# A recommendation tower: 17 gathered features instead of 16 in the first block, nine looked-up ones instead of ten

## What is computed

```python
combined = jnp.concatenate([dense_features[:, None, :], sparse_features], axis=1)   # (2048, 27, 128)
interactions = jnp.einsum('bfd,bgd->bfg', combined, combined)
interactions_flat = interactions[:, _IU0, _IU1]
z = jnp.concatenate([dense_features, interactions_flat], axis=1)
h = jnp.concatenate([z, r_dense_features], axis=1)
h = jnp.maximum(h @ W_top1 + b_top1, 0.0)
h = jnp.maximum(h @ W_top2 + b_top2, 0.0)
y = h @ W_top3
```

## Time and profile before

| | |
|---|---|
| median of 3 runs | 372.1 us (370.02 to 376.62) |
| the profiled execution's own time | 367.56 us |
| its span, first to last instruction | 365.8 us |
| PE busy | 339.0 us (93%) |
| DVE, POOL busy | 258.8 us each (71%) |
| ACT busy | 200.2 us (55%) |
| granted clock of PE, mean | 0.995 |

### The profile page before, as it was taken

How to read it: one execution, slowest core, us unless ns; L and a number is a source line. 1 busy time by engine, 2 the same in 40 slices (tenths; PEclk the granted TensorE clock), 3 DMA queues, 4 the chain that set the end, 5 groups by cost and what they waited for, 6 DMA issues and landing times.

```text
span 365.8 us, 8218 instructions
## 1 busy us (share of the span) xinstructions
PE 339.0 (93%) x3392; PEld 278.4 (76%) x3392; DVE 258.8 (71%) x190; ACT 200.2 (55%) x276; POOL 258.8 (71%) x268
## 2 busy tenths in 40 slices
PE   0889989999889799999999999999999999999987
PEld 0657668888778588888878688888877787868876
DVE  2969999899999979979787549878895221302132
ACT  2799995565549246654645454734636275734200
POOL 6778777777778777777777777777777777772220
PEclk9999999999999899999999999999999999999999
DMA  7998935599998559789535556787556431544310
GB/s 186 261 260 219 266 97 157 133 255 271 244 248 197 143 135 246 215 214 222 163 91 128 156 142 198 187 218 170 115 151 160 129 77 50 150 116 103 92 20 3
DMA packets 38034, 60.26 MB, mean 165 GB/s; under 512 B 20626, under 2 KB 21612, under 8 KB 37998
## 3 DMA queue, kind: packets, MB, share of 16 engines
q1 hardware_dynamic: 29046, 42.94, 44.8%
q0 software_dynamic: 8256, 16.42, 18.5%
q10 hardware_dynamic: 696, 0.38, 0.3%
HBM read 49.47 MB, written 10.23 MB: 163 GB/s over the span
## 4 chain that ended last, share of the span: by engine, by line
PE 67%; ACT 11%; SPq 8%; DMA 5%; issue 5%; DVE 4%; ACTq 0%; DVEq 0%
PE look_bank L790 29%; PE short_bank L887 13%; PE out_bank L821 8%; PE out_bank L837 6%; PE short_bank L872 5%; ACT one_hot L929 4%; PE out_bank L832 4%; ACT high_table L918 2%; SPq L656 2%; SPq L667 2%; DMA whole_table<-in_tbl 2%; ACT one_hot L936 2%; DVE one_hot L1111 2%; PE out_bank L849 1%; DMA block_scratch<-all_dots 1%
## 5 line engine op out<-in xcount | busy, mean ns | idle before, releaser
L730 POOL DMA_INDIRECT rows<-in_tbl,all_ids x248 | 251.8, 1015 | 77.1 <-issue 74.4
L1111 DVE TENSOR_TENSOR one_hot<-spread_ids,row_bank 128x2048 fp32r<-128x2048 int32 (+2 forms) x87 | 182.0, 2132 | 16.2 <-PE look_bank L790 11.9
L790 PE MATMUL look_bank<-one_hot,high_table 125*128 125x512 f32 x348 | 145.8, 419 | 18.2 <-DVE low_table L1099 11.3
L790 PE MATMUL look_bank<-one_hot,low_table 125*128 125x512 f32 x348 | 137.9, 396 | 0.0
L790 PEld LDWEIGHTS look_bank<-one_hot,high_table 125*128 125x128 f32 x348 | 66.7, 192 | 37.9 <-DVE low_table L1099 10.4
L790 PEld LDWEIGHTS look_bank<-one_hot,low_table 125*128 125x128 f32 x348 | 66.9, 192 | 15.7 <-issue 2.6
L887 PEld LDWEIGHTS short_bank<-all_combined 128*59 128x59 f32 x2048 | 57.9, 133 | 11.3 <-issue 9.7
L887 PE MATMUL short_bank<-all_combined 128*59 128x54 f32 x2048 | 60.7, 219 | 3.7 <-ACT all_combined L972 1.4
L1124 DVE COPY all_combined<-short_bank 128x512 f32<-128x512 f32 x32 | 21.7, 690 | 54.3 <-PE short_bank L872 54.0
L999 ACT COPY all_dots<-short_bank 128x432 f32<-128x432 f32 x64 | 32.7, 520 | 30.6 <-PE short_bank L887 26.5
L944 ACT COPY looked_up<-look_bank 128x512 f32<-128x512 f32 x42 | 24.7, 591 | 41.1 <-PE look_bank L790 40.9
(11 more groups left out here) (45 smaller groups left out, 185.5 us busy)
## 6 DMA issues: line engine op xcount, KB each, us to landing
whole_table<-in_tbl SPq DMA_DIRECT2D x27, 448.0 KB
spread_ids<-in_ids_by_feature SPq DMA_DIRECT2D x42, 256.0 KB, 5.9
block_scratch<-all_dots SPq DMA_DIRECT2D x24, 208.0 KB, 3.5
rows<-in_tbl,all_ids POOLq DMA_INDIRECT x248
block_scratch<-all_dots SPq DMA_DIRECT2D x24, 104.0 KB, 3.4
whole_table<-in_tbl SPq DMA_DIRECT2D x4, 560.0 KB
pairs<-block_scratch SPq DMA_DIRECT2D x72, 29.2 KB
whole_table<-in_tbl SPq DMA_DIRECT2D x27, 52.0 KB
```

Source lines behind the costliest of these rows:

```text
L730: nc.gpsimd.indirect_dma_start(rows[:, t % ROW_TILES, slot, :], None, tables[SLOT_FEATURES[slot]][:, :], bass.IndirectOffsetOnAxis(ap=all_ ...
L790: last = nc.tensor.matmul(look_bank[s % LOOK_BANKS][:], table_parts[part][TABLE_PLACE[s]][0:ROWS_K, c, :], one_hot[0:ROWS_K, (chunks_befor ...
L1111: last = nc.vector.tensor_tensor(one_hot[:, place:place + n, :], spread_ids[:, s % ID_PLACES:s % ID_PLACES + 1, :].to_broadcast([P, n, COLS]),
```

## The change

Block 0 gathers 17 features and looks up nine. The seventeenth makes a fifth group of a single transpose in the turns of tiles 0 to 3; ACT copies it. The list of look-ups is one shorter, so each later one has a number lower by one, while `ACT_HOTS` keeps its numbers. The search for tables that are still held is written anew. `y_sb` is laid over the start of `all_ids`, in the first tile's ids.

```diff
-GATHERED = [16, 15, 16, 15]
+GATHERED = [17, 15, 16, 15]
...
+def place_tables():
+
+    places, again, held = [], [], []
+    for s, f in enumerate(LOOK_FEATURE):
+        again.append(f in held)
+        places.append(held.index(f) if f in held else s if s < TABLE_PLACES else places[s - TABLE_PLACES])
+        held[places[s]:places[s] + 1] = [f]
+    return places, again
...
-GROUPS = [[4, 4, 4, 4], [4, 4, 4, 3], [4, 4, 4, 4], [4, 4, 4, 3]]
+GROUPS = [[4, 4, 4, 4, 1], [4, 4, 4, 3], [4, 4, 4, 4], [4, 4, 4, 3]]
...
-FIRST_MOVES = [8, 8, 8, 8]
+FIRST_MOVES = [7, 8, 8, 8]
...
+def by_dve(t, g):
+    return g % 2 == 0 and g < PER_BLOCK
...
+        with nc.sbuf_tensor("y_sb", [P, TILES], F32) as y_sb:
+            pass
         all_ids = sb("all_ids", [P, TILES, MOST_GATHERED], I32)
...
-                elif (before - turn_use(t, 0)) % 2 == 0:
-                    pe.wait_ge(even_copied, evens_by(t - 1) + (before - turn_use(t, 0)) // 2 + 1)
+                elif by_dve(t, before - turn_use(t, 0)):
+                    pe.wait_ge(turned_by_dve, by_dve_until(t - 1) + dve_groups(t).index(before - turn_use(t, 0)) + 1)
                 else:
-                    pe.wait_ge(odd_copied, odds_by(t - 1) + (before - turn_use(t, 0)) // 2 + 1)
+                    pe.wait_ge(turned_by_act, by_act_until(t - 1) + act_groups(t).index(before - turn_use(t, 0)) + 1)
...
-                        if g % 2 == 1:
+                        if not by_dve(t, g):
                             copy_group(t, g)
```

More of the change, by code:

```diff
@@ L53 @@
 SPLIT_AHEAD = 2
[L56 to L65, removed]
+def place_tables():
[5 more added lines that the diff above has]
+    return places, again
+TABLE_PLACE, AGAIN = place_tables()
 HIGH, LOW = range(2)
-GROUPS = [[4, 4, 4, 4], [4, 4, 4, 3], [4, 4, 4, 4], [4, 4, 4, 3]]
+GROUPS = [[4, 4, 4, 4, 1], [4, 4, 4, 3], [4, 4, 4, 4], [4, 4, 4, 3]]
 IN_QUAD = 4
@@ L154, in groups_by, with dve_groups, act_groups, by_dve_until @@
     return sum(n_groups(i) for i in range(t + 1))
[L157 to L164, removed]
+def by_dve(t, g):
+    return g % 2 == 0 and g < PER_BLOCK
+def dve_groups(t):
+    return [g for g in range(n_groups(t)) if by_dve(t, g)]
+def act_groups(t):
+    return [g for g in range(n_groups(t)) if not by_dve(t, g)]
+def by_dve_until(t):
+    return sum(len(dve_groups(i)) for i in range(t + 1))
+def by_act_until(t):
+    return sum(len(act_groups(i)) for i in range(t + 1))
 def turn_use(t, g):
@@ L453, in build @@
         bias2 = sb("bias2", [P, LAYER2])
-        y_sb = sb("y_sb", [P, TILES])
         block_scratch = [nc.dram_tensor(f"block_scratch{i}", (P, WRAPPED, PER_HALF * QUADS), F32).ap() for i in range(2)]
@@ L491, in build @@
         turned_done = sem("turned_done")
-        even_copied = sem("even_copied")
-        odd_copied = sem("odd_copied")
+        turned_by_dve = sem("turned_by_dve")
+        turned_by_act = sem("turned_by_act")
         dense_copied = sem("dense_copied")
@@ L875, in dot_tile @@
             def dot_tile(t):
-                pe.wait_ge(even_copied, evens_by(t))
-                pe.wait_ge(odd_copied, odds_by(t))
+                pe.wait_ge(turned_by_dve, by_dve_until(t))
+                pe.wait_ge(turned_by_act, by_act_until(t))
                 pe.wait_ge(dense_copied, t + 1)
@@ L989, in copy_group @@
                 to, of = group_views(t, g)
-                nc.scalar.copy(to, of).then_inc(odd_copied, 1)
+                nc.scalar.copy(to, of).then_inc(turned_by_act, 1)
             def copy_dots(t, b):
@@ L1123, in copy_group @@
                 to, of = group_views(t, g)
-                nc.vector.tensor_copy(to, of).then_inc(even_copied, 1)
+                nc.vector.tensor_copy(to, of).then_inc(turned_by_dve, 1)
             def copy_out(v, i):
@@ L1169, in _ @@
             made = make(0, 2 * LOOKS_BEFORE_TURN + 2)
-            for g in range(0, n_groups(0), 2):
+            for g in dve_groups(0):
                 copy_group(0, g)
@@ L1174, in _ @@
             for t in range(LAST * PER_BLOCK):
-                for g in range(0, n_groups(t + 1), 2):
+                for g in dve_groups(t + 1):
                     copy_group(t + 1, g)
```

## The result

The changed kernel takes **381.4 us** (median of 6 runs, 380.4 to 382.8) against 373.0 for the kernel before beside it (6 runs): a ratio of 1.0317, with a 95% interval of 1.0277 to 1.0357. The ratio counts for each kernel the runs near its fastest, and since the kernel before scatters more it lies above that of the medians, 1.023. Forecast were 383 and a range of 376 to 390. The profiled execution took 380.4 us, with a mean granted clock of 0.982 (before 367.56 and 0.995).

What follows compares the result with a forecast made beforehand. Bound: ACT's list in START, then PE from tile 0's dots on, passing any delay to the end. Terms 9.1 (START) + 0.1 + 2.1 (tiles 1 to 3) = 11.3 us, on the median 372.1: 383, range 376 to 390.

Steps and rivals of the forecast that it cites:

- The new wait: In START, PE stands 7.9 us before tile 0's fifth group until ACT has copied group 1, at 40.25.
- The clock behind it: After the 7.9 us pause in START, PE's matmuls run at a lower clock: 1.9 us lost, look-up 5 ends at 50.5.
- ACT's list: In START, ACT's last one-hot half ends at 64.2, PE pauses 3.3 us, tile 0's dots start at 68.6, 9.1 later.
- Tiles 1 to 3: Fourth group waits for DVE's copy: 0.1 us in tile 1; PE 1.4 late in tile 2; block 0 ends 2.1 later.
- The rest: From tile 4's dots, about 11 us late, to the end: same distances as before, nothing added.
- Gathers at nothing: Four more gathers put POOL 5 us later, covered by PE coming 11 us later; otherwise up to 5 could show.
- The new search and `y_sb`: Same tables held as before, and `y_sb` written long after tile 0's ids are read: both cost nothing.
- That the echoes are absent: Stall stays, but no clock fall in START or no delay from tiles 2 and 3: 7.8 to 9.2 us; chance 0.2.
- That ACT's list hides the wait: In START, PE's stand costs nothing if look-up 5 ends by about 42: dots at 58.1, 373 us; chance 0.08.
- That PE's work counts: PE, the busiest engine, has 3.2 us less work, so the whole takes 369 us; chance 0.05.
- More than 387: New DMA load or a deeper clock fall adds 4 to 8 us: 387 to 391; chance 0.09.
- Rival (2): Not slower: ACT sets the end of START and hides PE's stand; dots at 58.1, 373 us; chance 0.08.

Runs made afterwards that it cites:

- a_wait: Kernel before, plus only a wait of PE for ACT's copy of group 1 after the turns of tile 0: 379.7 us, ratio 1.0309.
- b: Changed kernel with the fifth turn of tile 0 moved behind the sixth look-up: 372.4 us, ratio 1.0116.
- d_warm: Changed kernel with 30 small identity matmuls, results unused, in PE's pause before the fifth group: 381.9 us, ratio 1.0365.
- g: Kernel before with the fourth group of turns right behind the third in tiles 1 to 3: 371.0 us, ratio 1.0046.
- j: Changed kernel without the four gathers of the 17th feature, its slot filled by two plain transfers: 382.0 us, ratio 1.0349.
- i: f_all without the four gathers of the 17th feature, its slot filled by two plain transfers: 366.8 us, ratio 0.9926.
- f_all: Changed kernel with fifth turn behind the sixth look-up, fourth groups behind the first four look-up steps, last one-hot half by DVE: 371.9 us, ratio 1.006.
- c: Changed kernel with the fourth group of turns of tiles 1 to 3 back behind the first four look-up steps: 380.6 us, ratio 1.0346.
- k: Kernel before with four more gathers that nobody reads, one behind each of tiles 0 to 3: 372.6 us, ratio 1.0079.
- e: Changed kernel with the second half of the ninth look-up made by DVE instead of ACT: 382.0 us, ratio 1.0339.
- h: Kernel before with the second half of look-up 8 made by DVE instead of ACT: 371.8 us, ratio 1.003.

## Why the prediction was right

**The new wait** (forecast: PE stands 7.9 us, released by ACT's copy at 40.25): 7.71 us, to 40.36. a_wait, which adds it, and b, which takes it away, show it to be the cause.

**The clock behind it** (1.9 lost, look-up 5 at 50.5): eight steps from 40.49 to 44.05 take 3.56 us instead of 1.86, 1.7 lost; ACT has the look-up's end at 50.65. d_warm gives 1.4 for it at tile 0.

**ACT's list** (last half ready at 64.2, a pause of 3.3, dots at 68.6): 64.20, 2.82 and 68.70. **At tile 0 the sum was 9.1 and the trace has 9.2.** The walk in start-to-start times came out because it followed both lists, ACT's and PE's, wherever one waits for the other. Small errors in it cancel: PE was 0.6 us later at the last pause than forecast, which the pause took up, and the distance of 0.95 from the last matmul's end to the dots is 0.86 by the earlier trace rows (58.41 and 0.23).

**Tiles 1 to 3** (0.1 and 2.1): 0.2 at tile 1 and 2.8 at tile 4, where the sum has 2.2. The stands of 1.4 are 1.40 and 1.73, and the pause behind tile 3 does end with DVE's low part (at 124.38 before and 136.35 changed, each 0.1 us ahead of PE). The mechanism stands, by g; the size is 0.6 too small. The working also left out a stand: at 95.45 the kernel before waits 1.15 us within tile 2's dot products, in a slice with an 8 of the earlier trace rows, and in the changed kernel that wait is gone. So the second stand costs less than it shows: from the dots of tile 2 to those of tile 3 the changed kernel loses 0.7 us (19.84 against 19.14), which is 1.73 - 1.15 and a transpose of 0.12. It loses 1.8 from tile 1 to tile 2.

**The rest** (same distances to the end): 0.8 more, in three steps of 0.1 to 0.4 behind tile 8. No step had it. The mean granted clock of the six timed runs of the changed kernel is 0.972 to 0.982, and steps of this size also come and go between executions (below); which of them belong to the change stays open.

**Gathers at nothing**, as PE is 11 us later, "were PE on time, up to 5 us could show": j gives 0, i against f_all 5. The new search and `y_sb` were priced at nothing too. No run changes them alone, but a_wait has the loss of `START` without them, and i has them and is faster than the kernel before.

**The rivals.** That the echoes are absent is refuted by tile 4. That ACT's list hides the wait failed on its own point: look-up 5 ended at 50.65, not by 42. That PE's work counts: PE has less to do and the kernel is slower; with the waits for ACT and DVE mended, f_all is still 0.6% slower than the kernel before, and only i, which leaves four gathers out, is 0.7% faster. More than 387 didn't come.

**The number.** That the median came within 1.6 us of the forecast is in part luck, since two errors oppose each other: between the profiled executions lie 12.8 us where I had 11.3, but I put my sum on a median 4.5 above its profile, and the changed kernel's median is only 1.0 above its own.

One part I saw too simply. Rival (2), the change without the cost of its wait, had dots at 58.1 and 373 us, next to nothing. b is that case, with dots at 59.82 and 1.2% slower: the sum left out the slow matmuls behind a pause of 2.83 us. And where f_all mends that too, the gathers come forward.

## What to carry to other kernels

When a group is added to a rotation of banks, the question is not how much work it is but whose copy frees the bank it takes, and what that engine has queued ahead of the copy: here one transpose of 0.1 us cost 9 us. A copy that nobody waits for may stand anywhere in an engine's list; on the day somebody does, its place is on the critical path. And work that was priced at nothing because an engine is late (here four gathers) gets its price back as soon as the lateness is mended, so the repair has to be reckoned with it.

## What the runs showed of the hardware

**The same pause lowers the clock in one trace and not in another.** Before the look-ups behind tile 3, PE pauses 2.41 us in the kernel before, 2.37 in the changed one, 2.40 in b, 2.41 in c, 2.19 in k, and each time matmuls 0.43 us apart follow (in c only from the seventh on); it pauses 2.39 in e, 2.40 in h, 2.27 in d and 2.18 in j, and they stay 0.23 us apart. It is worth 1.5 us: from the dots of tile 3 to those of tile 4 are 20.8 to 21.1 us with it and 19.4 to 19.5 without. Pauses of 7.7 and 2.8 us were always followed by slow matmuls in these traces, those of 1.1 to 1.2 us in `START` never.

**Near the dot products the clock also fell with hardly a pause.** In i the matmuls of the look-up are 0.43 us apart from 212.36 on (granted clock 1.00 from 210 to 212 us, 0.57 from 212 to 216), though PE has only stood 0.20 us ahead of them; what came before were a tile's dot products, turns and the last layer's 128x1 matmuls. PE's timeline:

```profile
210.16 0.66 PE L896 MATMUL short_bank<-identity,rows 128*128 128x128 f32 x4 [0.20 <-issue]
210.65 1.84 PE L873 MATMUL out_bank<-w,hidden 128*128 128x1 f32 x16
212.36 0.64 PE L814 MATMUL look_bank<-one_hot,high_table 125*128 125x512 f32 x1
212.79 0.63 PE L814 MATMUL look_bank<-one_hot,low_table 125*128 125x512 f32 x1
```

In e the same happens behind 0.84 us at 224.40, and the granted clock is 0.63 in the next window; from the dots of tile 8 to those of tile 9 it needs 25.7 us, the changed kernel 22.3. That one, behind 0.28 and 0.22 us, keeps its clock, and so does a_wait behind 0.80 us; that the pause is what decides isn't shown. The window of e:

```profile
225.00:230.00 5.00, 5.00 (x24) 0.63 0.74 216
```

**The scatter of the runs goes with the clock.** The traces above are one of each kernel, but executions of one kernel differ in the same way. Of 23 timed runs of the kernel before beside i, the three with a mean granted clock of 1.000 took 367.3 to 369.6 us and the eight with 0.989 to 0.991 took 369.7 to 372.5. Whether the clock makes all of this difference isn't shown.

So one profiled execution carries 1.5 us behind tile 3 that need not belong to its kernel, and more at two other places: over all traces the way from the dots of tile 8 to those of tile 9 takes 21.5 to 25.7 us, and that from tile 14 to tile 15 13.9 to 17.5 (in the longer of these PE waits for transfers too). Differences of this size are safe only tile by tile, away from these places, or by many timed runs.

**Identity matmuls in a pause kept the clock** (d_warm, 1.00 instead of 0.50), but they brought back only what the clock had cost at that place, 1.4 us of 9.2, and the whole time didn't fall.
